# A fused transformer and graph-attention kernel: partial-array products made whole, probability buffers per tile, and a new step order

## The reference

```python
# layer 0, a conditioned transformer block
mods = silu(c) @ adaln_w + adaln_b            # six rows of 256 per sequence
x_mod = rms(x) * (1 + scale_msa) + shift_msa
q, k, v = split(x_mod @ qkv_w)                # 16 heads of 16
q, k = rope(rms(q, lnq_w), rms(k, lnk_w))
x = x + gate_msa * (softmax(q k^T / 4) v @ proj_w + proj_b)
h = rms(x) * (1 + scale_mlp) + shift_mlp
x = x + gate_mlp * ((silu(h @ w1_w) * (h @ w3_w)) @ w2_w)   # width 704
# layer 1, a graph attention over the 64 rows, 20 of them as keys
self_feat = concat(x, c, or 0 where sum(x) == 0) @ W_self.T + b_self
for d in 0, 1:                                # two directions of the edges
    aff = where(sum(adj_d) > 0, q_d k_d^T / 4, -9e15) + adj_d @ w_bias + b_bias
    output += softmax(aff) (self_feat[:, :20]) @ Wout[d] + bout[d]
x = x + relu(self_feat + output)
```

## Time and profile before

| | us |
|---|---|
| three runs | 1419.06, 1424.35, 1425.61 |
| median | 1424.35 |
| the profiled execution, its own time | 1418.18 |
| span from its first to its last instruction | 1416.1 |
| mean granted clock of the PE | 0.977 |

### The profile page before, as it was taken

The page is one execution under the profiler, slowest core; times in us unless marked ns, Lnnn a source line. Parts: engine busy times, 40 slices in busy tenths (PEclk is TensorE's granted clock), DMA queues, the critical chain, the costliest instruction groups (busy, mean ns, idle before and its releaser), DMA issues.

```text
span 1416.1 us, 51305 instructions
## 1 busy us (share of the span) xinstructions
PE 1342.2 (95%) x20276; PEld 1229.1 (87%) x20276; DVE 1135.2 (80%) x2033; ACT 878.6 (62%) x1752; POOL 712.1 (50%) x612
## 2 busy tenths in 40 slices
PE   4679999999999999999999999999999999999985
PEld 3578899999998999999898999999999999999974
DVE  5667888888888888888888888888888888888753
ACT  4556666666666666666666666666666666656542
POOL 0235555455655544555555455555545555554541
PEclk8589999999999999999999999999999999999998
DMA  7001111010111101111110111111011111100100
GB/s 240 29 23 30 45 43 43 18 38 30 43 43 43 43 15 36 34 43 43 43 43 15 35 35 43 43 43 43 15 33 37 43 43 43 43 15 28 30 22 16
DMA packets 49827, 56.19 MB, mean 40 GB/s; under 512 B 4352, under 2 KB 47744, under 8 KB 49792
## 3 DMA queue, kind: packets, MB, share of 16 engines
q1 hardware_dynamic: 48944, 53.86, 12.1%
q10 hardware_dynamic: 848, 1.84, 0.4%
HBM read 47.03 MB, written 8.65 MB: 39 GB/s over the span
## 4 chain that ended last, share of the span: by engine, by line
PE 73%; issue 9%; POOL 7%; ACT 3%; DVE 1%; ACTq 0%; POOLq 0%; DVEq 0%
PE psum L486 39%; PE psum L607 5%; PE psum L622 5%; PE psum L728 4%; PE psum L792 4%; PE psum L758 4%; PE psum L775 3%; POOL nl L1315 3%; PE psum L587 3%; PE psum L806 2%; POOL gl L1315 2%; POOL kbd L1327 2%; ACT gh L926 1%; PE psum L534 1%; ACT qkT L892 1%
## 5 line engine op out<-in xcount | busy, mean ns | idle before, releaser
L1315 POOL TENSOR_TENSOR gl<-gf,gh 128x512 fp32r<-128x512 f32 x96 | 124.3, 1295 | 260.4 <-ACT gh L926 260.4
L486 PE MATMUL psum<-nh,w_lo 128*128 128x256 f32 x704 | 182.2, 289 | 0.0
L486 PE MATMUL psum<-nh,w_hi 128*128 128x256 f32 x704 | 176.8, 282 | 0.0
L1315 POOL TENSOR_TENSOR nl<-xn,nh 128x512 fp32r<-128x512 f32 x64 | 99.2, 1551 | 127.3 <-ACT nh L864 127.3
L486 PEld LDWEIGHTS psum<-nh,w_lo 128*128 128x128 f32 x704 | 132.8, 189 | 1.0 <-issue 1.0
L486 PEld LDWEIGHTS psum<-nh,w_hi 128*128 128x128 f32 x704 | 133.0, 189 | 0.0
L1379 POOL TENSOR_TENSOR e<-e,inv 128x640 f32<-128x640 f32 x64 | 82.0, 1282 | 87.6 <-DVE inv L1271 87.6
L486 PE MATMUL psum<-nl,w_hi 128*128 128x256 f32 x704 | 115.4, 282 | 0.0
L926 ACT ACTIVATE gh<-gf 128x512 fp32r<-128x512 f32 x96 | 60.3, 628 | 61.6 <-DVE gf L1201 60.8
L486 PEld LDWEIGHTS psum<-nl,w_hi 128*128 128x128 f32 x704 | 97.5, 188 | 0.0
L486 PE MATMUL psum<-qkv_lo,nh 128*128 128x512 f32 (+1 forms) x256 | 88.5, 356 | 2.8 <-ACT nh L864 2.8
(11 more groups left out here) (186 smaller groups left out, 4382.4 us busy)
## 6 DMA issues: line engine op xcount, KB each, us to landing
adj<-in_adj SPq DMA_DIRECT2D x32, 440.0 KB, 3.3
x_in<-in_x SPq DMA_DIRECT2D x32, 256.0 KB, 2.7
xn<-in_xT SPq DMA_DIRECT2D x32, 256.0 KB, 3.6
x_res<-in_xT SPq DMA_DIRECT2D x32, 256.0 KB, 3.7
out_T<-y SPq DMA_DIRECT2D x32, 256.0 KB, 2.2
e<-in_adaln ACTq DMA_DIRECT2D x2, 512.0 KB, 5.4
stage<-in_qkv SPq DMA_DIRECT2D x2, 384.0 KB, 5.0
pT<-in_w SPq DMA_DIRECT2D x2, 384.0 KB, 6.4
```

The costliest lines, as they stand in the source:

```text
L486: last = nc.tensor.matmul(out, lhsT, rhs, start=start and i == 0, stop=stop and i == len(terms) - 1)
L1315: return nc.gpsimd.tensor_tensor(out, full, hi.bitcast(F32), ALU.subtract)
```

## The change

- `mlp_down`: the last chunk is made whole. w2 is passed with its last 64 rows twice, on both halves of the partitions; POOL writes the low part of g on partitions 0 to 63 of gh's last chunk, beside the high part on 64 to 127. So two products for each output half (W_lo and W_hi) in place of three 64-row ones. POOL's last low part becomes two instructions, of 128 and of 64 partitions by 256.
- `self_cond`: `gate` and `cond_rows` are 128 rows, zero but for the first 8, so the two products use all rows.
- `probsT`: the transposed probabilities of layer 0 go into `e0` of the same tile, those of layer 1 into one half of `pT` for each tile. `score` on DVE now waits for `mix` of the block before instead of for its transposes.
- `score1_bias`: one instruction of 640 elements for each tile; `score1` on PE writes the scores in the order that this needs.
- All five lists of `ORDER`, the banks, and the waits for free banks are new. The cut of the loop stands elsewhere (after `k1` on PE), which is no change of order by itself.
- Prologue: the steps of block 0 no longer wait for the condition rows and the rope tables; DVE makes these behind the first `norm0_shift`, and the wait stands ahead of `qkv` on PE and, for four of the modulation rows, ahead of `norm0_scale` on POOL. Two memsets are added on DVE.

```diff
 BANK = {
-    "xT": 6, "qk": (2, 3), "v": (7, 1), "heads": (7, 5), "probsT": (5, 4, 4, 0), "probsT1": (0, 5, 4, 7),
-    "mix": (5, 6), "q1": (4, 6), "score": 0, "score1": 0, "mixT": 6, "proj": 2, "norm1": 7, "up": (6, 4, 6),
-    "gate": (3, 1, 0), "down": 1, "rowsum": 3, "self": 4, "k1": 5, "v1": 7, "mix1": 5,
+    "xT": 1, "qk": (2, 5), "v": (1, 6), "heads": (5, 4), "probsT": (0, 7, 3, 4), "probsT1": (4, 0, 5, 7),
+    "mix": (0, 3), "q1": (0, 6), "score": 2, "score1": 3, "mixT": 6, "proj": 2, "norm1": 7, "up": (2, 6, 7),
+    "gate": (0, 5, 2), "down": 2, "rowsum": 5, "self": 1, "k1": 6, "v1": 1, "mix1": 1,
 }
     "PE": [
-        (2, "heads", 1), (1, "proj", 0), (0, "self", 0), (0, "self_cond", 0), (2, "score", 0), (0, "k1", 0),
-        (0, "q1", 0), (1, "norm1_mean", 0), (0, "q1", 1), (1, "norm1_apply", 0), (2, "probsT", 0),
-        (3, "norm0_apply", 0), (0, "score1", 0), (0, "v1", 0), (2, "mix", 0), (2, "probsT", 1), (1, "mlp_up", 0),
-        (1, "mlp_up", 1), (3, "qkv", 0), (0, "probsT1", 0), (2, "mix", 1), (3, "qkv", 1), (0, "mix1", 0),
-        (0, "probsT1", 1), (1, "mlp_up", 2), (0, "mix1", 1), (1, "mlp_down", 0), (1, "mlp_down", 1), (2, "mixT", 0),
-        (3, "heads", 0),
+        (1, "norm1_mean", 0), (0, "q1", 0), (1, "norm1_apply", 0), (0, "q1", 1), (3, "norm0_apply", 0),
+        (2, "probsT", 0), (0, "score1", 0), (1, "mlp_up", 0), (2, "probsT", 1), (1, "mlp_up", 1), (3, "qkv", 0),
+        (2, "mix", 0), (2, "mix", 1), (1, "mlp_up", 2), (3, "qkv", 1), (0, "v1", 0), (0, "probsT1", 0),
+        (0, "probsT1", 1), (1, "mlp_down", 0), (0, "mix1", 0), (0, "mix1", 1), (1, "mlp_down", 1), (2, "mixT", 0),
+        (3, "heads", 0), (3, "heads", 1), (2, "proj", 0), (1, "self", 0), (1, "self_cond", 0), (3, "score", 0),
+        (1, "k1", 0),
     ],
     "DVE": [
...
+        (1, "norm1_shift", 0), (3, "norm0_apply", 0), (1, "edges", 0), (0, "score1_bias", 0), (0, "score1_bias", 1),
+        (3, "norm0_shift", 0), (0, "score1_max", 0), (1, "mlp_up", 0), (0, "score1", 0), (0, "score1_max", 1),
+        (1, "mlp_up", 1), (0, "score1", 1), (0, "soft1", 0), (3, "qkv", 0), (2, "mix", 0), (0, "soft1_inverse", 0),
+        (2, "mix", 1), (0, "soft1", 1), (0, "soft1_inverse", 1), (1, "mlp_up", 2), (3, "qkv", 1),
+        (1, "edge_masks", 0), (3, "rope_scale", 0), (3, "rope", 0), (3, "rope", 1), (0, "mix1", 0), (0, "out", 0),
+        (1, "mlp_down", 0), (2, "mixT", 0), (2, "proj", 0), (1, "row_mask", 0), (3, "score_max", 0),
+        (2, "norm1_squares", 0), (3, "score", 0), (2, "norm1_mean", 0), (1, "k1", 0), (3, "score_max", 1),
+        (2, "norm1_apply", 0), (3, "score", 1),
     ],
...
     "SP": [
-        (0, "self", 0), (3, "norm0_mean", 0), (1, "mlp_up", 0), (3, "norm0_scale", 0), (2, "norm0_apply", 0),
+        (1, "mlp_up", 0), (3, "norm0_mean", 0), (3, "norm0_scale", 0), (0, "self", 0), (1, "norm0_apply", 0),
         (0, "out", 0),
     ],
...
-        pT0, pT1 = pT[:, 0, :, :], pT[:, 1, :, :]
+        pT0 = [v[:, :, :].rearrange("p h s -> p (h s)").rearrange("p (j t) -> p j t", t=P) for v in e0]
+        pT1 = [pT[:, t, :, :] for t in range(TILES)]
...
-        gate = sb("gate", [2 * MB, MT], F32R)
-        cond_rows = sb("cond_rows", [2 * MB, D], F32R)
+        gate = sb("gate", [P, MT], F32R)
+        cond_rows = sb("cond_rows", [P, D], F32R)
...
             def mlp_down(m, n):
...
                 for o in both:
-                    for i, (w, a) in enumerate(((wl["w2"], gh), (wh["w2"], gh), (wh["w2"], gl))):
-                        last = nc.tensor.matmul(down_ps[:, o, :], w[half, MC - 1, out_chunks[o]], a[half, MC - 1, :],
-                                                start=False, stop=o == DC - 1 and i == 2, tile_position=(HALF, 0))
+                    last = linear(down_ps[:, o, :], high_terms("w2", out_chunks[o], gh, [MC - 1]), False, o == DC - 1)
                 last.then_inc(down_done.sem, 1)
...
             def probs_t(m, t):
-                if isinstance(m, int) and m == 0:
-                    act.wait_ge(weight_lo.sem, 5)
-                wait(act, pT_ps, m, 2 * t + 1)
-                wait(act, mixed, m, t)
-                nc.scalar.activation(pT0[:, 0:4, :], pT_out[t][0], ACT.Copy).then_inc(pT_a.sem, 1)
                 wait(act, pT_ps, m, 2 * t + 2)
-                nc.scalar.activation(pT0[:, 4:8, :], pT_out[t][1], ACT.Copy).then_inc(pT_b.sem, 1)
+                nc.scalar.activation(pT0[t][:, 0:4, :], pT_out[t][0], ACT.Copy).then_inc(pT_a.sem, 1)
+                nc.scalar.activation(pT0[t][:, 4:8, :], pT_out[t][1], ACT.Copy).then_inc(pT_b.sem, 1)
...
             def score1_bias(m, t):
...
-                for a in range(ND):
-                    nc.vector.tensor_tensor(
-                        e1[t][:, :, a, 0:NKV].rearrange("p (r h) k -> p r h k", r=NG),
-                        s1_ps[t].rearrange("p r (a h k) -> p r a h k", a=ND, k=NKV)[:, :, a, :, :],
-                        edge_bias[:, t, a * NKV:(a + 1) * NKV].unsqueeze(1).unsqueeze(1).to_broadcast([P, NG, 4, NKV]), ALU.add)\
-                        .then_inc(biased1.sem, 1)
+                nc.vector.tensor_tensor(
+                    e1[t][:, :, :, 0:NKV].rearrange("p (r h) a k -> p r h a k", r=NG), s1_v[t],
+                    edge_bias[:, t, :].rearrange("p (a k) -> p a k", a=ND).unsqueeze(1).unsqueeze(1).to_broadcast([P, NG, 4, ND, NKV]),
+                    ALU.add).then_inc(biased1.sem, 1)
...
             def mlp_up(m, n):
                 wait(pool, g_hi, m, n + 1)
-                low_part(gl[:, 2 * n:2 * n + 2, :], gf[:, :, :], gh[:, 2 * n:2 * n + 2, :]).then_inc(g_lo.sem, 1)
+                if n < MC // 2 - 1:
+                    low_part(gl[:, 2 * n:2 * n + 2, :], gf[:, :, :], gh[:, 2 * n:2 * n + 2, :]).then_inc(g_lo.sem, 1)
+                else:
+
+                    low_part(gl[:, 2 * n, :], gf[:, 0, :], gh[:, 2 * n, :]).then_inc(g_lo_whole.sem, 1)
+                    wait(pool, g_lo_whole, m, 1)
+                    low_part(gh[0:HALF, 2 * n + 1, :], gf[HALF:, 1, :], gh[HALF:, 2 * n + 1, :]).then_inc(g_lo.sem, 1)
+                    wait(pool, g_lo, m, n + 1)
...
-        "w2": np.insert(a["L0_cond_w2_w"], [HM - HALF] * HALF, 0, 0),
+        "w2": np.concatenate([a["L0_cond_w2_w"], a["L0_cond_w2_w"][HM - HALF:]], 0),
```

More of the change, by code:

```diff
@@ L88 @@
+        (1, "k1", 0),
     ],
     "DVE": [
-        (2, "rope", 0), (2, "rope", 1), (0, "mlp_down", 0), (1, "mixT", 0), (1, "proj", 0), (0, "row_mask", 0),
-        (0, "edge_masks", 0), (2, "score_max", 0), (2, "score", 0), (1, "norm1_squares", 0), (2, "score_max", 1),
[4 rows of a table removed]
-        (1, "mlp_up", 1), (2, "mix", 1), (3, "qkv", 0), (3, "qkv", 1), (1, "mlp_up", 2), (0, "mix1", 0),
-        (1, "edges", 0), (3, "rope_scale", 0), (0, "out", 0),
[3 rows of a table added]
+        (2, "mix", 1), (0, "soft1", 1), (0, "soft1_inverse", 1), (1, "mlp_up", 2), (3, "qkv", 1),
@@ L101 @@
-        (0, "x2_split", 0), (0, "self", 0), (1, "norm1_mean", 0), (0, "keys", 0), (0, "self_split", 0),
-        (3, "norm0_mean", 0), (2, "score", 0), (0, "q1", 0), (0, "q1", 1), (2, "probsT", 0), (2, "score", 1),
-        (1, "norm1_apply", 0), (0, "v1", 0), (3, "norm0_apply", 0), (1, "edges", 0), (0, "score1", 0),
-        (2, "probsT", 1), (1, "mlp_up", 0), (1, "mlp_split", 0), (0, "score1", 1), (1, "mlp_up", 1),
-        (0, "probsT1", 0), (3, "qkv", 0), (1, "mlp_split", 1), (3, "qkv", 1), (0, "probsT1", 1), (1, "mlp_up", 2),
+        (3, "norm0_mean", 0), (0, "self_split", 0), (2, "score", 0), (0, "q1", 0), (0, "q1", 1),
@@ new lines @@
+        (1, "norm1_apply", 0), (2, "score", 1), (2, "probsT", 0), (1, "mlp_up", 0), (3, "norm0_apply", 0),
+        (1, "mlp_split", 0), (1, "edges", 0), (1, "mlp_up", 1), (2, "probsT", 1), (0, "score1", 0),
+        (1, "mlp_split", 1), (3, "qkv", 0), (0, "keys", 0), (0, "score1", 1), (1, "mlp_up", 2), (3, "qkv", 1),
+        (1, "mlp_split", 2), (0, "v1", 0), (3, "rope_scale", 0), (0, "probsT1", 0), (0, "probsT1", 1), (2, "mixT", 0),
+        (3, "heads", 0), (3, "heads", 1), (1, "x2_split", 0), (1, "self", 0), (2, "norm1_mean", 0),
@@ L106 @@
     ],
     "Pool": [
[L108 to L111 removed]
+        (0, "x2_split", 0), (2, "heads", 1), (1, "proj", 0), (1, "norm1_scale", 0), (0, "self_split", 0),
@@ L112 @@
+        (1, "norm1_mean", 0), (3, "norm0_mean", 0), (3, "norm0_scale", 0), (1, "norm1_apply", 0),
+        (3, "norm0_apply", 0), (1, "mlp_up", 0), (1, "mlp_up", 1), (0, "soft1", 0), (0, "soft1", 1), (1, "edges", 0),
+        (1, "mlp_up", 2), (1, "mlp_down", 0), (3, "heads", 0),
     ],
     "SP": [
-        (0, "self", 0), (3, "norm0_mean", 0), (1, "mlp_up", 0), (3, "norm0_scale", 0), (2, "norm0_apply", 0),
+        (1, "mlp_up", 0), (3, "norm0_mean", 0), (3, "norm0_scale", 0), (0, "self", 0), (1, "norm0_apply", 0),
@@ L676, in mlp_down @@
                 first_use(m, "w2")
-                half = slice(HALF, P)
                 if n == 0:
@@ L1011, in _ @@
```

(2 more changed lines are left out.)

161 lines of the change are left out of this document (82 added, 79 removed), and 4 rows, old and new, of the table ORDER.

## The result

The changed kernel takes 1446.28 us (median of four runs, 1440.88 to 1452.65), the kernel before beside it on the same chip 1423.18: a ratio of 1.0167, 95% interval 1.0114 to 1.022. The forecast was 1416 with 1392 to 1437 around it. It is slower, by 1.7%, and outside the range.

The account below looks back on a forecast made before the run. PE's own instruction stream was taken to bound the loop. Removed PE work -30.7, waits at mlp_up and cond_rows 31 x (0.5 + 0.3), prologue -2.2: -8.1 us, giving 1416 us, range 1392 to 1437.

Parts of the forecast that it names:

- the loop is bound by the PE's own instruction stream: Whole loop: PE busy 41.07 of 41.42 us per block, so PE savings count fully if other engines deliver in time.
- What is removed on the PE: PE work per block: tail, condition rows and shape changes together save 0.96 us, 30.7 us for 32 blocks.
- The tail: End of mlp_down: four whole products replace six 64-row ones, saving 0.54 us per block (0.45 to 0.60), two shape changes included.
- The condition rows: The two self_cond gate products: using whole rows saves 0.12 us per block (0 to 0.30).
- the third term: Shape changes from score1 to v1 and v1 to mix: two fewer save 0.30 us per block (0 to 0.6).
- the term at mlp_up: mlp_up now comes early, so PE waits for POOL's low part nl: 0.5 us per block (0 to 1.1).
- in the second half of the pass, behind qkv: Sign that the prediction is wrong at the root: PE waits arising there.
- cond_rows: Fetch now queued behind store, edges, x_in and xT: PE waits 0.3 us per block (0 to 0.8).
- x_res: Issued last, may land about 1 us late for POOL's x1; hidden by DVE's score maximum, priced at nothing.
- The filling: Prologue: norm freed of the condition rows saves 2 us (0 to 3.5); the sum uses -2.2.
- Rival B: SP's queue: late cond_rows and x_res plus a long mlp_up path cost +0.4 to +0.6 per block; 1436 us, chance 0.24.
- DVE and POOL beside each other: POOL's nl for mlp_up: 1.68 us beside a two-SBUF-operand DVE instruction, 1.29 otherwise; if held up, 12 us more.

Follow-up runs that it names:

- e6: Kernel before, only mlp_down's six 64-row tail products made four 128-row ones on PE (a low part left out), POOL's low part unchanged: 1421.25 us, period 41.41.
- e19: e12 with the second kbd (spreading of k) moved from POOL to DVE and the low part of x2 ahead of POOL's remaining one: 1407.0 us, ratio 0.9892.
- e12: Changed kernel with cond_rows and x_res fetched a block earlier, DVE's mlp_down ahead of y, and y reading ACT's copy of x2: 1411.11 us, period 41.28.
- e17: e16 with POOL's low part of x2 (nl) ahead of both spreadings of k (kbd): 1416.53 us, period 41.50.
- e16: e12 with y one instruction later on DVE, POOL's order as it was: 1418.64 us, period 41.51.
- e4: Kernel before in its own order, with only mlp_down's last chunk and the condition rows made whole-array products: 1428.6 us, ratio 1.0066.
- e1: Changed kernel with SP fetching cond_rows and x_res of the next block as soon as their buffers are free: 1414.22 us, ratio 0.9942.
- e11: Kernel before with the 128-row tail on PE (a low part left out) and y moved late on DVE, without adding x2: 1428.68 us, period 41.50.
- e3: Changed kernel with both fetches a block earlier and DVE's mlp_down ahead of y, addition of x2 to the output left out: 1411.36 us, period 41.25.
- e10: Changed kernel with only x_res fetched a block earlier, cond_rows left where the change put it: 1425.1 us, ratio 1.0029.
- e7: e6 with DVE's 1.06 us sum over adj moved out of its chain from sf to mlp_down: 1421.85 us, period 41.40.
- e2: Changed kernel with DVE's mlp_down ahead of y, addition of x2 to the output left out, fetches not moved: 1547.97 us, ratio 1.0848.
- e5: Changed kernel with only cond_rows asked for a block earlier, x_res of this block standing behind that fetch on SP: 1585.84 us, ratio 1.1141.
- e14: e11 with POOL's low part of x2 (nl) ahead of both spreadings of k: 1448.74 us, ratio 1.0223.

## Why the prediction was wrong

**That the loop is bound by the PE's own instruction stream, and other engines answer only at mlp_up.** This is the step that failed at the root. The share of 95% is true and says that the PE hardly waits; it does not say that a second line is not just as long. The prediction had named the condition, that every other engine still brings its part in time, and worked it out for one path only; removed work on the PE was priced at its full worth. e6 isolates it: 0.51 us taken from the PE, 0.51 back at the row of ones, period unchanged. In the order of before the line is DVE's row from gf over y and rope to the gating (or gl and then y, when that is longer), POOL's x2, ACT's split, and behind them POOL's nl and two kbd, with score at the end. In the changed order it starts at the sums of mix1: y, gating, x2, split. The list of waits of before gives no sign of it, since two lines of equal length look like one engine that never waits; the timeline does, as the high part of x2 is done 0.05 us before the PE reads it. e19 supports it from the other side: against e12 it moves one kbd from POOL to DVE and puts nl ahead of the other, leaves the PE's list as it was, and shortens the block by 0.24 us, 0.22 of it at the low products of self. The order alone gave nothing with y late (e17 against e16), which speaks for the work taken off POOL as what lets it pay.

**What is removed on the PE.** The tail was right: 0.51 measured in e6, 0.54 forecast. Two products fewer are 0.24 of it, which leaves 0.27 for the two changes of shape, as the prediction had it. The condition rows were not: nothing in e4, against 0.12. In the changed order the gate pair with score behind it takes 0.43 instead of 0.54, about the 0.12, but since e4 has the same product without that gain, it goes with the neighbours (score now uses other banks and starts otherwise), not with the rows. The two changes of shape around v1, the third term, no run isolates, and no run isolates the buffers per tile or the merged bias add either. In all, the products' slots that got shorter from the kernel before to e1 add up to 1.4 us per block, waits that were inside them among them, more than the 0.96 forecast.

**What comes back.** Those that got longer add up to 1.4 as well: proj with the row of ones behind it 0.43, heads and the bank that proj shares with the down product 0.17, the transposes ahead of score1 0.28 (score1 waits for DVE's e), mlp_up 0.22, and 0.31 in small pieces. Only the first of these is tied to its cause by experiments (e6, e11, e3); the others are read from the slots and waits. The line of score1 in e1's list of waits:

```profile
PE psum L780 <- DVE e L1165: 7.8, 29, 0.3
```

So the term at mlp_up, 0.5 with POOL's nl as the cause, was mis-sized. It is 0.2 in e1. About 0.12 of that is nl: there nl ends at 661.40 and its first weight load begins at 661.45, 0.14 late. In the changed kernel, where x_res has already held up q1, even that is gone, and mlp_up takes 0.1 more than before. Part of what came back stands one step ahead, at score1, and most of the rest in proj and heads: waits of the PE "in the second half of the pass, behind qkv", which the text had named as the sign that it is wrong at the root.

**cond_rows.** The mechanism and the bounds were right: wait 0.3 taken, 0 to 0.8 as bounds, 0.44 us per block measured. With T = 698.56, the end of y in this period, the PE was ready near T+5.6 (forecast T+5.35) and the product started at T+6.4, after 0.77 us of wait; the transfer behind the three others was due at T+6.0 to 6.1 at the latest, and the last of the three landed at T+6.2. The Trainium skill, "DMA: Bandwidth & Descriptors", section "Queues, rings and completion order", has each transfer engine take the descriptors of one issuing engine's row in ring order, which speaks for that late landing. The trace agrees: the product started 0.23 us after the last of the three had landed.

**x_res.** That it "may land about 1 us late" but is hidden by DVE's score maximum is the transfer term that failed. POOL's x1 starts at T+6.9; the squares and the mean are 0.2 us later for it than in e10, and the first q1, whose low part POOL makes behind x1, takes 0.4 more. It costs 0.41 us per block (e10 against the changed kernel), and was priced at nothing.

**Sum.** Forecast per block: -0.96 + 0.5 + 0.3 = -0.16. Measured: -1.4 + 1.4 (what came back, the second line's share in it) + 0.44 (cond_rows) + 0.41 (x_res) = +0.85, against 0.82 by the two periods, which times 30 is 25 us, less about 3 in the filling. The filling was forecast at -2 (the sum has -2.2) and measured at -3.5. Rival B had named both transfers and their place, at 1436. It still ended 10 us short. It had 1.55 for the transfers and the path to mlp_up, where the transfers cost 0.85, and took off 0.96 for the PE, of which the loop kept nothing, and up to 0.2 as hidden: errors that partly cancelled.

**DVE and POOL beside each other.** The prediction weighed such a pair on one row (1.68 against 1.29) and for nl only. By the runs it decides at another place: y is issued beside gl and ends only 0.54 us behind it (e7), and x2 on POOL takes 1.61 us beside y (e3). The Trainium skill, "SBUF — State Buffer", section "SBUF: two separate sides", has a DVE instruction with two SBUF inputs and a POOL instruction that reads SBUF shut each other out. The trace agrees nearly in full: gl had 1.06 us to run when y was issued, and y took 0.98 longer.

## What to carry to other kernels

Before a saving on a busy engine is priced at its full length, follow the line of the other engines from its last inputs to the next step that reads them: if it arrives just in time, the saving is worth nothing until that line is shortened too. The test is cheap: shorten the engine's work alone and see at which instruction the wait comes back; if turning the order on a second engine only moves the wait to the next reader, that engine has to do less. And place a small transfer by when its reader asks, not behind large ones that nobody waits for yet; two fetches a block ahead cost one line here and were worth 0.85 us per block.

## What the runs showed of the hardware

The PE's clock: in e2, after 1.67 us without work, the granted clock was 0.52 over the next 7.6 us, close to the lower of its two levels (1.2 of 2.4 GHz), with products 0.21 us apart, and 1.00 again later; in e5, after 3.34 us, 0.50:

```profile
712.00:721.00 9.00, 8.22 (x115) 7.25 (x111) 5.04 (x10) 2.69 (x5) 4.54 (x4) 1.00 0.43 137
727.81:732.00 4.19, 4.19 (x19) 4.19 (x20) 3.46 (x7) 3.03 (x5) 3.72 (x5) 0.50 0.00 0
```

In the period shown of the changed kernel a wait of 0.77 us left it at 1.00, but a short wait is no safe side: in three blocks of e14 the clock stood at 0.50 for 6.8 us (284.47 to 291.29 in one of them) and the block was 2.9 us longer, with no wait of the PE in them over 0.92 us, while its other blocks, with waits of 0.7 to 0.9, stayed at 1.00. In e5 it takes 6.1 us on average from the start of the mean to the end of the second q1, where e1 needs 3.8: the long wait cost 2.3 us more than itself.

A product over 8 rows and one over 128 cost the same here, entry and exit included (0.540 and 0.546 us for the pair, in the order of before), so filling these rows up with zeros neither cost nor gained.

A DVE instruction with two operands in SBUF and a POOL instruction hardly overlapped: whichever came second was longer by most of what the first had still to run (y 0.63 to 1.60 behind gl, kbd 1.04 to 1.51 and x2 1.31 to 1.61 behind y). DVE's sum over adj, with one operand, ran beside gl with both at their usual length (1.06 and 1.30 in e6).
